# Cross-attention and a quantized feed-forward block: the feed-forward's quantized values turned by VectorE squares and a DMA through device memory instead of by TensorE

## The chip, the cores and the metric

The kernel runs on one core of a Trainium2 chip. The metric is the device time of one execution in microseconds (us); lower is better. Before the change the median of three executions is 2209.33 us (2207.35 to 2211.3).

## The reference, cut to what matters

```python
x = x + xattn(layernorm(x), ctx, ctx, Wq, bq, Wk, bk, Wv, bv, Wo, bo)   # x: 16 x 224 x 512, ctx: 16 x 750 x 512, 16 heads
x = x + ffn(layernorm(x), w_gate, w_up, w_down)

def fp4_quant_dequant(x):            # blocks of 16 along the last dimension
    scale = maximum(max(abs(xb)) / 6.0, 1e-12)
    idx = searchsorted(_MID, abs(xb / scale))
    return _GRID[idx] * sign(xb / scale) * scale

def fp4_linear(x, w):
    return einsum('bsk,nk->bsn', fp4_quant_dequant(x), fp4_quant_dequant(w))

def ffn(x, w_gate, w_up, w_down):    # 512 -> 1408 -> 512
    h = silu(fp4_linear(x, w_gate)) * fp4_linear(x, w_up)
    return fp4_linear(h, w_down)
```

## The kernel before, in words

The program has two stages, each a block of five instruction streams that run at their own pace and meet at semaphores. The first is the cross-attention over 16 batches (0 to about 1497 us in the trace); it also quantizes the three feed-forward weights and keeps gate and up turned and split in SBUF. The second is the feed-forward, `feed_forward`, over 28 tiles of 128 rows. All matrix products are made of three passes over operands that are split in a high and a low part (`PASSES`), so each operand is needed twice: the high part is written by ScalarE (a copy to float32r), the low part by VectorE (the value less the high part).

TensorE needs the quantized values with the contracted dimension on the partitions, so they are turned: the normed and quantized x of a tile (512 columns, 4 squares of 128) and the quantized hidden values (1408 columns, 11 squares of 128). Before the change TensorE turns them with an identity matrix into PSUM (`turn_x`, lines 1154 to 1162, and `turn_h`, lines 1185 to 1196), ScalarE copies the high parts out of `turn_bank` (lines 1216 to 1219 and 1233 to 1240), and VectorE subtracts (lines 1296 to 1299 and 1309 to 1315).

The order of work is written out by hand. `period_units(n)` gives the units of period n, and each engine walks that list and carries out what concerns it. In period n TensorE makes gate and up of tile n in three chunks of 512, 512 and 384 columns (`gate_up`, 24 matmuls a chunk) and the down product of tile n - 2 (`down`, 33 matmuls); VectorE quantizes in one pass of nine steps (`quant`, `quantize_step`) the hidden values of tile n - 1 together with the normed x of tile n + 2, 1920 columns in all, and between these steps makes the norm of tile n + 3, the hidden product of tile n (`hidden`, three chunks), the low parts, and the sum with the residual (`store`). ScalarE makes the silu of each chunk and the high parts. SyncE issues the transfers: `load` of a tile of x, `load_res` of the residual, `store` of the output. The banks for gate and up are two each, so `gate_up` of a chunk waits for the `hidden` of the chunk before the last one.

What a unit waits for can be said in counts: `gate_up(n, 0)` waits for `x_lo` of tile n, `down(n - 2, c)` for the low part of that chunk, `hidden(n, c)` for the silu, step 1 of `quant(n)` for `hidden(n - 1, 2)`.

Periods 3 to 24 are a hardware loop of two periods a turn (line 1096), the first three and the last five are written out. In periods 0 and 1 TensorE also turns the down weights.

## Time and profile before

| | before |
|---|---|
| median of three executions | 2209.33 us |
| the profiled execution's own time | 2209.99 us |
| its span, first to last instruction | 2208.2 us |
| PE busy | 2125.9 us (96%) |
| DVE busy | 1626.9 us (74%) |
| ACT busy | 866.9 us (39%) |
| feed-forward, from its first gate matmul | 1498.1 us to the end |
| granted TensorE clock, mean | 0.988 |

The page divides the span into 40 slices and shows for each engine its busy tenths; the timeline lists instructions in order of their start, neighbours of one kind merged; the windows sum busy time over a stretch. PE is the matmul part of TensorE, DVE is VectorE, ACT is ScalarE, SPq is the queue in which SyncE issues transfers. A start of one row less the start of the row before tells the pace, since neighbouring instructions overlap a little. "Landing" of a transfer is counted from its issue.

### The profile page before, as it was taken

How to read it: one execution, taken by the hardware profiler on the slowest of the kernel's cores; microseconds unless marked ns; L12 is line 12 of the kernel's file. 1: busy time of each engine (PE TensorE's matmuls, PEld its weight loads, DVE VectorE, ACT ScalarE, POOL GpSimd, SP SyncE). 2: the span in 40 equal slices, each digit the busy share in tenths (PEclk: the TensorE clock that was granted, in tenths of full speed). 3: DMA queues.
4: the chain of work that ended last, by engine and by line, in shares of the span. 5: the costliest groups of instructions: out<-in, count | busy, mean ns of one | idle time of the engine just before them, and what ended most of it. 6: DMA issues, size and time to landing. Idle time of an engine off the chain costs nothing. (4 is left out here: it accounts for less than half of the span.)

```text
span 2208.2 us, 43977 instructions
## 1 busy us (share of the span) xinstructions
PE 2125.9 (96%) x17252; PEld 1840.0 (83%) x17252; DVE 1626.9 (74%) x2818; ACT 866.9 (39%) x1805; POOL 96.5 (4%) x162
## 2 busy tenths in 40 slices
PE   4999999999999999999999999679999999999998
PEld 4888888888888988888889888558888888888886
DVE  4777777777777777776777777477878787788865
ACT  4554555455454554554545455342111111111111
POOL 0000000000000000000000000000000000000000
PEclk9999999999999999999999999879999999999999
DMA  5344444534434445345344444433000100010000
GB/s 163 102 113 105 124 106 122 136 94 116 131 94 123 104 122 132 98 120 136 93 118 105 122 124 104 109 103 95 29 28 28 43 28 28 28 39 33 24 20 29
DMA packets 124012, 197.24 MB, mean 89 GB/s; under 512 B 29776, under 2 KB 72272, under 8 KB 121280
## 3 DMA queue, kind: packets, MB, share of 16 engines
q1 hardware_dynamic: 123840, 194.86, 32.6%
q8 instruction: 118, 1.93, 0.4%
q14 instruction: 54, 0.44, 0.1%
HBM read 75.67 MB, written 23.33 MB: 45 GB/s over the span
## 5 line engine op out<-in xcount | busy, mean ns | idle before, releaser
L692 DVE TENSOR_REDUCE row_max<-max_bank 128x1 f32<-128x376 f32 (+1 forms) x896 | 450.7, 537 | 186.9 <-PE max_bank L523 186.5
L602 ACT ACTIVATE probs<-score_bank 125x448 f32<-125x448 f32 x768 | 399.5, 541 | 292.6 <-PE score_bank L537 289.8
L475 PE MATMUL proj_bank<-attention_operands 128*128 128x376 f32 (+1 forms) x1536 | 290.3, 338 | 24.5 <-DVE attention_operands L734 18.9
L497 PE MATMUL proj_bank<-attention_operands 128*128 128x256 f32 x2304 | 305.6, 283 | 6.1 <-DVE wo_lo L811 6.1
L537 PE MATMUL score_bank<-qstack,kstack 103*128 103x224 f32 x1536 | 301.0, 282 | 1.5 <-DVE qstack L703 1.3
L497 PEld LDWEIGHTS proj_bank<-attention_operands 128*128 128x128 f32 x2304 | 289.9, 190 | 6.4 <-DVE wo_lo L811 6.4
L537 PEld LDWEIGHTS score_bank<-qstack,kstack 103*128 103x128 f32 x1536 | 256.9, 192 | 37.8 <-issue 35.9
L475 PEld LDWEIGHTS proj_bank<-attention_operands 128*128 128x128 f32 x1536 | 264.1, 191 | 26.0 <-issue 18.9
L1231 ACT ACTIVATE f_act_gate<-gate_bank 128x512 f32<-128x512 f32 (+1 forms) x84 | 47.2, 562 | 504.4 <-PE up_bank L1181 504.4
L1181 PE MATMUL gate_bank<-gate_up,early 128*128 128x512 f32 (+1 forms) x1008 | 233.7, 381 | 1.5 <-PEq L1352 1.5
L1181 PE MATMUL up_bank<-gate_up,early 128*128 128x512 f32 (+1 forms) x1008 | 228.8, 376 | 0.0
L552 PE MATMUL pv_bank<-probs,values 125*32 125x224 f32 x3072 | 221.1, 360 | 0.0
L558 PE MATMUL pv_bank<-probs,ones 125*32 125x224 f32 x3072 | 217.2, 355 | 0.0
L1206 PE MATMUL down_bank<-ffn_down_hi,f_hqt 128*128 128x512 f32 x616 | 205.6, 400 | 6.5 <-DVE f_hqt L1314 6.5
L1181 PEld LDWEIGHTS up_bank<-gate_up,early 128*128 128x128 f32 x1008 | 184.9, 188 | 30.6
L1181 PEld LDWEIGHTS gate_bank<-gate_up,early 128*128 128x128 f32 x1008 | 181.0, 188 | 29.6 <-issue 2.0
L1307 DVE TENSOR_TENSOR f_hidden<-f_act_gate,up_bank 128x512 f32<-128x512 f32 (+1 forms) x84 | 54.0, 642 | 136.1 <-ACT f_act_gate L1231 136.1
L741 DVE RECIPROCAL heads<-pv_bank 128x112 f32<-128x112 f32 x128 | 108.6, 850 | 50.9 <-PE pv_bank L558 50.9
L1206 PEld LDWEIGHTS down_bank<-ffn_down_hi,f_hqt 128*128 128x128 f32 x616 | 116.6, 189 | 33.5 <-DVE f_hqt L1314 7.3
L558 PEld LDWEIGHTS pv_bank<-probs,ones 125*32 125x32 f32 x3072 | 100.4, 111 | 47.0 <-issue 2.0
L523 PE MATMUL max_bank<-early 128*128 128x376 f32 x448 | 131.7, 347 | 4.1 <-ACT early L640 2.3
L552 PEld LDWEIGHTS pv_bank<-probs,values 125*32 125x32 f32 x3072 | 87.3, 110 | 55.1 <-issue 19.0
(126 smaller groups left out, 2773.5 us busy)
## 6 DMA issues: line engine op xcount, KB each, us to landing
ctx_raw<-in_ctx SPq DMA_DIRECT2D x16, 1500.0 KB, 7.7
kstack<-k_low SPq DMA_DIRECT2D x256, 93.8 KB, 2.2
kstack<-early SPq DMA_DIRECT2D x256, 93.8 KB, 2.2
kstack<-k_high SPq DMA_DIRECT2D x256, 93.8 KB, 2.2
qstack<-early SPq DMA_DIRECT2D x384, 28.0 KB, 1.9
qstack<-q_part SPq DMA_DIRECT2D x384, 28.0 KB, 1.8
ffn_quant<-fw_share SPq DMA_DIRECT2D x48, 176.0 KB, 2.1
xn<-in_x SPq DMA_DIRECT2D x16, 448.0 KB, 9.9
```

What stands on the lines that cost most here:

```text
L475: last = nc.tensor.matmul(out[:, 0:hi - lo], w_hi_lo[W_K][ws][:, c, g * P:(g + 1) * P], ctx_part[cs][:, c, lo:hi], start=(n == 0), stop=(n ...
L497: last = nc.tensor.matmul(out[:, 0:256], ctx_part[cs][:, c, kt * KW:kt * KW + P], w_hi_lo[W_V][ws][:, c, half * 256:(half + 1) * 256], sta ...
L523: nc.tensor.matmul(out[:, 0:hi - lo], masked_columns[t % 2][:, m * P:(m + 1) * P], k_part[t % 2][0][:, lo:hi], start=True, stop=True).then ...
L537: last = nc.tensor.matmul(score_bank[j % 2][:, k * SQ:(k + 1) * SQ], kstack[t % 2][0:STK, j, kt * KW:kt * KW + P], qstack[t % 2][:, j, :], ...
L552: last = nc.tensor.matmul(pv_bank[j * DK:(j + 1) * DK, 0:SQ], values[:, t % NG // 2, kt, col:col + DK], probs[p][:, j, k, :], start=(kt == ...
L558: last = nc.tensor.matmul(pv_bank[j * DK:(j + 1) * DK, SQ:2 * SQ], ones[0:KW, :], probs[p][:, j, k, :], start=False, stop=(kt == KT - 1), ...
L602: nc.scalar.activation(probs[p][:, j, :, :], score_bank[j % 2][0:KW, 0:2 * SQ].rearrange("p (k q) -> p k q", k=2), ACT.Exp, scale=float(DK ...
L692: nc.vector.tensor_reduce(row_max[:, m, kh:kh + 1], mbank[:, 0:KSPLIT[kh + 1] - KSPLIT[kh]], AX.X, ALU.max).then_inc(max_reduced, 1)
L741: nc.vector.reciprocal(heads[:, half], pv_bank[:, SQ + half.start:SQ + half.stop])\
L1181: last = nc.tensor.matmul(banks[par][:, 0:w], xqt[n % 2][xs_][:, kc, :], ffn[m][ws][:, kc, chunk(c)], start=(k == 0), stop=(k == 11))
L1206: last = nc.tensor.matmul(down_bank[n % 2][:, :], hqt[hs][:, m, :], ffn[2][ws][:, m, :], start=(m == 0 and k == 0), stop=(m == FC - 1 and ...
L1307: nc.vector.tensor_tensor(hidden[:, chunk(c)], act_gate[par][:, 0:w], up_bank[par][:, 0:w], ALU.mult).then_inc(hidden_done, 1)
```

## The change

In the feed-forward's steady periods the turning leaves TensorE. After the ninth step of `quant(n)`, VectorE turns `quantized` in squares of 32 by 32 in one instruction into `strips` (unit `strips`). SyncE stores `strips`, 128 partitions of 1920 values, to a scratch in device memory, waits until it is there, and loads it back with four transfers of 32 partitions each into `turned`, so that the squares come to stand where the turned matrix has them (unit `bounce`). In the next period ScalarE makes the high parts from `turned` (`x_hi`, `h_hi`) and VectorE the low parts (`x_lo`, `h_lo`), both with SBUF as source instead of PSUM. `strips`, `turned` and the high and low parts of h are single buffers; the scratch has two.

The order in a period changes with it: the high parts stand at its head, the low parts behind the fourth step of `quant`, `hidden(n, 0)` behind the seventh, `hidden(n, 1)` and `strips` behind the ninth; TensorE makes all three chunks of `gate_up(n)` and then the three of `down(n - 2)`. All tiles are written out, with no hardware loop. The last two periods (28 and 29) turn by TensorE as before (`tail_units`). In the attention a table with explicit places replaces a sum of floats for the masks of q; the only effect is that in one of four slots a mask of q and `heads_hi` change places on ScalarE.

```diff
@@ period_units
-    return [*when(3, ("load", n + 3)), *when(0, ("gate_up", n, 0)), *quant(1, 2),
-            *when(-3, ("store", n - 3)), *quant(3, 4), *when(-1, ("load_res", n - 1)),
-            *when(1, ("turn_x", n + 1)), *when(-2, ("turn_h", n - 2, 0, has(1))),
-            *when(3, ("norm", n + 3)), *when(0, ("hidden", n, 0), ("gate_up", n, 1)),
-            *quant(5), *when(1, ("turn_x_lo", n + 1)), *quant(6), *when(-2, ("turn_h_lo", n - 2, 0)),
-            *when(-2, ("turn_h", n - 2, 1, has(1)), ("down", n - 2, 0), ("turn_h", n - 2, 2, has(1))),
-            *quant(7), *when(0, ("hidden", n, 1)), *when(-2, ("turn_h_lo", n - 2, 1)),
-            *when(3, ("normalize", n + 3)), *when(0, ("gate_up", n, 2)), *quant(8),
-            *when(-2, ("turn_h_lo", n - 2, 2)),  *when(0, ("hidden", n, 2)),
-            *when(-2, ("down", n - 2, 1), ("down", n - 2, 2)), *quant(9)]
+    spread = [("strips", n, has(-1), has(2))] if has(-1) or has(2) else []
+    bounce = [("bounce", n, has(-1), has(2))] if has(-1) or has(2) else []
+    return [*when(3, ("load", n + 3)), *when(1, ("x_hi", n + 1)), *when(-2, *[("h_hi", n - 2, c) for c in range(3)]),
+            *when(0, ("gate_up", n, 0)), *quant(1, 2, 3, 4),
+            *when(-2, *[("h_lo", n - 2, c) for c in range(3)]), *when(1, ("x_lo", n + 1)),
+            *quant(5, 6), *when(3, ("norm", n + 3)), *quant(7), *when(0, ("hidden", n, 0), ("gate_up", n, 1)),
+            *when(-3, ("store", n - 3)), *when(-1, ("load_res", n - 1)), *quant(8), *when(3, ("normalize", n + 3)), *quant(9),
+            *when(0, ("hidden", n, 1), ("gate_up", n, 2)), *(spread if last_spread is None or n <= last_spread else []),
+            *when(-2, *[("down", n - 2, c) for c in range(3)]), *when(0, ("hidden", n, 2)),
+            *(bounce if last_spread is None or n <= last_spread else [])]
...
@@ feed_forward
+    WC = W // P
+    in_squares = quantized[:, :].rearrange("p (k c j) -> p c k j", c=HG, j=DK)
+    strips = sb("f_strips", [P, HG, WC, DK])
+    turned = sb("f_turned", [P, HG, WC, DK])
...
-        with engine.Fori(1, tiles // 2 - 2) as i:
+        for i in range(1, tiles // 2 - 2):
             body(i, period_units(1) + period_units(2))
-        for n in range(1, 6):
-            body(tiles // 2 - 2, period_units(n, left=4 - n))
+        for n in range(1, 4):
+            body(tiles // 2 - 2, period_units(n, left=4 - n, last_spread=2))
+        for n in range(4, 6):
+            body(tiles // 2 - 2, tail_units(n))
...
@@ sync
+                elif kind == "bounce":
+                    part = chunks_of(*_rest)
+                    there = strips_dram[n % 2]
+                    sp.wait_ge(strips_made, tile + 1)
+                    reached(sp, turned_loaded, 16 * HG * (tile - 1))
+                    sp.dma_start(there.rearrange("p (c k j) -> p c k j", c=HG, j=DK)[:, :, part, :],
+                                 strips[:, :, part, :]).then_inc(strips_stored, 16)
+                    sp.wait_ge(strips_stored, 16 * (tile + 1))
+                    sp.wait_ge(x_lo, tile + 2)
+                    reached(sp, h_lo, 3 * (tile - 1))
+                    for c in range(HG):
+                        sp.dma_start(turned[c * DK:(c + 1) * DK, :, part, :], there.rearrange(
+                            "(g i) (c k j) -> c i g k j", i=DK, c=HG, j=DK)[bass.ds(c, 1), :, :, part, :].rearrange(
+                                "a i g k j -> (a i) g k j")).then_inc(turned_loaded, 16)
...
@@ scalar
+                if kind == "x_hi":
+                    act.wait_ge(turned_loaded, 16 * HG * (tile - 1))
+                    reached(act, gated, 3 * (tile - 1))
+                    nc.scalar.activation(in_strips(xqt[n % 2][0]), turned_chunks(FC, WC),
                                          ACT.Copy).then_inc(x_hi, 1)
+                elif kind == "h_hi":
+                    c = rest[0]
+                    q = 3 * tile + c
+                    if c == 0:
+                        act.wait_ge(turned_loaded, 16 * HG * (tile + 2))
+                        act.wait_ge(down_turned, FC)
+                    reached(act, down_part, q - 2)
+                    lo, hi = CH[c] // P, CH[c + 1] // P
+                    nc.scalar.activation(in_strips(hqt[0][:, lo:hi, :]), turned_chunks(lo, hi),
+                                         ACT.Copy).then_inc(h_hi, 1)
...
@@ vector
+                elif kind == "strips":
+                    part = chunks_of(*rest)
+                    dve.wait_ge(q_steps, quant_count(tile + 2, QSTEPS))
+                    reached(dve, strips_stored, 16 * tile)
+                    nc.vector.transpose(strips[:, :, part, :], in_squares[:, :, part, :]).then_inc(strips_made, 1)
+                elif kind == "x_lo":
                     dve.wait_ge(x_hi, tile + 1)
+                    nc.vector.tensor_tensor(in_strips(xqt[n % 2][1]), turned_chunks(FC, WC),
+                                            in_strips(xqt[n % 2][0]).bitcast(F32), ALU.subtract).then_inc(x_lo, 1)
+                elif kind == "h_lo":
+                    c = rest[0]
+                    dve.wait_ge(h_hi, 3 * tile + c + 1)
+                    lo, hi = CH[c] // P, CH[c + 1] // P
+                    nc.vector.tensor_tensor(in_strips(hqt[1][:, lo:hi, :]), turned_chunks(lo, hi),
+                                            in_strips(hqt[0][:, lo:hi, :]).bitcast(F32), ALU.subtract).then_inc(h_lo, 1)
```

VectorE's order from one period into the next, the kernel before, near its end (`f_q_steps` are the nine steps, L982 the ninth, L967, L969, L971 and L973 the first four, L1319 the sum with the residual):

```order
L982 TENSOR_TENSOR f_quantized<-f_round,f_scale 128x1920 [waits f_h_turned,f_x_turned,f_q_steps]
L967 TENSOR_REDUCE f_amax<-f_hidden 128x88 [waits f_hidden_done]
L969 TENSOR_SCALAR f_scale<-f_amax 128x88 [waits f_q_steps]
L1319 TENSOR_TENSOR f_res<-down_bank,f_res 128x512 [waits f_res_loaded1,f_down_part]
L971 RECIPROCAL f_inv_scale<-f_scale 128x88 [waits f_q_steps]
L973 SCALAR_TENSOR_TENSOR f_scaled<-f_hidden,f_inv_scale 128x1408 [waits f_q_steps]
```

The same place in the changed kernel, in a steady period (L986 is the ninth step, L971 the first, L979 the fifth, L1356 and L1350 the low parts, L1365 `hidden`; the waited names are in the diff):

```order
L986 TENSOR_TENSOR f_quantized<-f_round,f_scale 128x1920 [waits f_strips_made,f_q_steps]
L1365 TENSOR_TENSOR f_hidden<-f_act_gate,up_bank 128x512 [waits f_silu_done]
L1347 STREAM_TRANSPOSE f_strips<-f_quantized 128x1920 [waits f_strips_stored,f_q_steps]
L1365 TENSOR_TENSOR f_hidden<-f_act_gate,up_bank 128x384 [waits f_silu_done]
L971 TENSOR_REDUCE f_amax<-f_hidden 128x120 [waits f_hidden_done,f_x_normed]
L973 TENSOR_SCALAR f_scale<-f_amax 128x120 [waits f_q_steps]
L975 RECIPROCAL f_inv_scale<-f_scale 128x120 [waits f_q_steps]
L977 SCALAR_TENSOR_TENSOR f_scaled<-f_hidden,f_inv_scale 128x1920 [waits f_q_steps]
L1356 TENSOR_TENSOR f_hqt<-f_turned,f_hqt 128x512 [waits f_h_hi] x2
L1356 TENSOR_TENSOR f_hqt<-f_turned,f_hqt 128x384 [waits f_h_hi]
L1350 TENSOR_TENSOR early<-f_turned,early 128x512 [waits f_x_hi]
L979 TENSOR_SCALAR f_power<-f_scaled 128x1920 [waits f_q_steps]
```

Between the transpose and the first low part stand one `hidden` and four steps; before, no such instruction existed, and the low parts stood one by one between later steps.

SyncE's queue in a steady period of the changed kernel (L1179 the store of the strips, L1185 the four loads, L1160 the load of x, L1190 the output, L1172 the residual):

```order
L1179 DMA strips_scratch<-f_strips 128x1920 [waits f_turned_loaded,f_strips_made]
L1185 DMA f_turned<-strips_scratch 32x4x480 [waits f_h_lo,f_x_lo,f_strips_stored]
L1185 DMA f_turned<-strips_scratch 32x4x480 x3
L1160 DMA f_xn<-x_scratch 128x512 [waits f_x_normed]
L1190 DMA out<-f_res 128x512 [waits f_y_done]
L1172 DMA f_res<-x_scratch 128x512 [waits f_stored0]
```

ScalarE's queue over one period of the changed kernel (L1255 `x_hi`, L1265 `h_hi`, L1278 the silu):

```order
L1255 ACTIVATE early<-f_turned 128x512 [waits f_gate_up_made,f_turned_loaded]
L1265 ACTIVATE f_hqt<-f_turned 128x512 [waits f_down_part,f_down_turned,f_turned_loaded]
L1265 ACTIVATE f_hqt<-f_turned 128x512 [waits f_down_part]
L1265 ACTIVATE f_hqt<-f_turned 128x384 [waits f_down_part]
L1278 ACTIVATE f_act_gate<-gate_bank 128x512 [waits f_hidden_done,f_gate_up_made] x2
L1278 ACTIVATE f_act_gate<-gate_bank 128x384 [waits f_hidden_done,f_gate_up_made]
```

The five new transfers stand ahead of the load of x in SyncE's queue, and the two high parts that used to wait for TensorE's turning now wait for `turned_loaded`.

## Rows read from the trace of the kernel before

**Rows 1.** Page, part 2: TensorE and its clock in 40 slices of the span.
```profile
PE   4999999999999999999999999679999999999998
...
PEclk9999999999999999999999999879999999999999
```

**Rows 2.** Windows, steady part: stretch, busy us (instructions) by engine, clock, DMA share, GB/s.
```profile
1650.00:1700.00 50.00, 50.00 (x244) 42.21 (x243) 39.93 (x44) 7.35 (x14) 1.48 (x4) 1.00 0.10 31
```

**Rows 3.** Timeline, PE, one period: start us, us, engine, line, what, shapes, count.
```profile
1808.46 2.96 PE L1181 MATMUL gate_bank<-gate_up,early 128*128 128x512 f32 x12
1811.26 2.97 PE L1181 MATMUL up_bank<-gate_up,early 128*128 128x512 f32 x12
...
1824.03 2.33 PE L1181 MATMUL gate_bank<-gate_up,early 128*128 128x384 f32 x12
1826.19 2.24 PE L1181 MATMUL up_bank<-gate_up,early 128*128 128x384 f32 x12
...
1833.17 1.10 PE L1181 MATMUL gate_bank<-gate_up,early 128*128 128x512 f32 x4
```

**Rows 4.** Timeline, DVE, the same period.
```profile
1806.83 2.15 DVE L967 TENSOR_REDUCE f_amax<-f_hidden 128x120 f32<-128x1920 f32 x1
1809.01 0.22 DVE L969 TENSOR_SCALAR f_scale<-f_amax 128x120 f32<-128x120 f32 x1
...
1809.85 0.89 DVE L971 RECIPROCAL f_inv_scale<-f_scale 128x120 f32<-128x120 f32 x1
1810.78 2.16 DVE L973 SCALAR_TENSOR_TENSOR f_scaled<-f_hidden,f_inv_scale 128x1920 f32<-128x1920 f32 x1
1812.86 0.68 DVE L1264 BATCH_NORM_STATS2 f_stats<-f_xn 128x6 f32<-128x512 f32 x1
...
1815.67 1.15 DVE L975 TENSOR_SCALAR f_power<-f_scaled 128x1920 uint32<-128x1920 uint32 x1
1816.74 0.68 DVE L1298 TENSOR_TENSOR early<-turn_bank,early 128x512 fp32r<-128x512 f32 x1
1817.34 1.15 DVE L977 TENSOR_SCALAR f_power<-f_power 128x1920 f32<-128x1920 f32 x1
```

**Rows 5.** Timeline, ACT, the same period.
```profile
1815.32 0.61 ACT L1239 ACTIVATE f_hqt<-turn_bank 128x512 fp32r<-128x512 f32 x1
```

**Rows 6.** Groups by form, 100 to 1400: busy us, mean ns | idle before, releaser.
```profile
L734 DVE TENSOR_TENSOR attention_operands<-ctx_raw,attention_operands 128x750 fp32r<-128x750 f32 x60 | 52.4, 936 | 3.8 <-ACT attention_operands L633 3.8
...
L633 ACT ACTIVATE attention_operands<-ctx_raw 128x750 fp32r<-128x750 f32 x60 | 44.8, 818 | 0.4
```

**Rows 7.** DMA issues by line: KB each, median us from issue to landing.
```profile
ctx_raw<-in_ctx SPq DMA_DIRECT2D x16, 1500.0 KB, 7.7
kstack<-k_low SPq DMA_DIRECT2D x256, 93.8 KB, 2.2
...
f_res<-x_scratch SPq DMA_DIRECT2D x28, 256.0 KB, 2.6
out<-f_res SPq DMA_DIRECT2D x28, 256.0 KB, 2.0
...
values<-in_wk SPq DMA_DIRECT2D x1, 1024.0 KB, 6.1
```

**Rows 8.** Windows in a burst of 32-partition DMAs: us, DVE busy, clock, DMA share, GB/s.
```profile
124.00:126.00 2.00, 1.46 (x3) 1.00 0.65 152
...
140.00:142.00 2.00, 1.66 (x3) 1.00 0.56 203
```

**Rows 9.** Timeline, DVE, end of period 1.
```profile
1536.74 2.15 DVE L982 TENSOR_TENSOR f_quantized<-f_round,f_scale 128x1920 f32<-128x1920 f32 x1
```

**Rows 10.** Timeline, PE, last tiles' gate_up in period 27.
```profile
2169.48 2.34 PE L1181 MATMUL gate_bank<-gate_up,early 128*128 128x384 f32 x12
```

**Rows 11.** Timeline, PE, in the tail, behind an idle stretch.
```profile
2184.30 0.80 PE L1206 MATMUL down_bank<-ffn_down_hi,f_hqt 128*128 128x512 f32 x1 [4.63 <-DVE f_hqt L1314]
```

**Rows 12.** Windows, the stretch behind that idle time: columns as in Rows 2.
```profile
2184.00:2188.00 4.00, 3.70 (x9) 2.92 (x10) 3.91 (x4) 0.00 (x0) 0.00 (x0) 0.50 0.00 0
```

More of the change, by code:

```diff
@@ L73 @@
         "q": 7.96,
+        "mask": (8.26, 8.96, 9.66, 10.36),
         "q_lo": 8.16,
@@ L97 @@
         "q": 8.06,
+        "mask": (8.36, 9.06, 9.76, 10.46),
         "q_lo": 8.5,
@@ L121 @@
         "q": 8.7,
+        "mask": (9.0, 9.7, 10.4, 11.1),
         "q_lo": 11.71,
@@ L145 @@
         "q": 4.22,
+        "mask": (4.52, 5.22, 5.92, 6.62),
         "q_lo": 4.26,
@@ L226, in slot_units @@
         add(at["q_lo"], ("q_lo", g + 2))
-        add((at["q"] + 0.3, at["q"] + 1.0, at["q"] + 1.7, at["q"] + 2.4), *[("mask_q", g + 2, j) for j in range(HG)])
+        add(at["mask"], *[("mask_q", g + 2, j) for j in range(HG)])
         ahead, half = g // 2, 1 - g // 2
@@ L982, in quantize_step, with period_units @@
     return dve.tensor_tensor(blocks(out), blocks(t), spread(scale), ALU.mult)
-def period_units(n, first=None, left=None):
+def period_units(n, first=None, left=None, last_spread=None):
     def has(k):
@@ L1031, in with_down, with feed_forward @@
     return out + [("down_turn_lo", i) for i in turns if ("down_turn_lo", i) not in out]
-def feed_forward(nc, ctx, x1, out, ffn, ident, ln_consts, tiles, ffn_quant, xqt, fs):
+def feed_forward(nc, ctx, x1, out, ffn, ident, ln_consts, tiles, ffn_quant, strips_dram, xqt, fs):
     def sb(name, shape, dt=F32):
@@ L1153, in body @@
                 tile = 2 * i + n
-                if kind == "turn_x":
-                    reached(pe, q_steps, quant_count(tile, QSTEPS))
-                    reached(pe, x_lo, tile)
-                    reached(pe, h_lo, 3 * (tile - 4) + 2)
-                    for c in range(KC):
-                        col = F + c * P
-                        last = nc.tensor.transpose(turn_bank[0][:, c * P:(c + 1) * P], quantized[:, col:col + P],
-                                                   ident[:, :])
-                    last.then_inc(x_turned, 1)
-                elif kind == "down_turn":
+                if kind == "down_turn":
                     pe.wait_ge(down_loaded[n % RAWS], 16 * (n // RAWS) + 16)
@@ L1185, in body @@
                 elif kind == "turn_h":
-                    c, after_x = rest
+                    c = rest[0]
                     q = 3 * tile + c
-                    reached(pe, q_steps, quant_count(tile + 3, QSTEPS))
-                    reached(pe, h_lo, q - 1 if c else q)
-                    if c == 1 and after_x:
-                        reached(pe, x_lo, tile + 4)
+                    pe.wait_ge(q_steps, quant_count(tile + 3, QSTEPS))
+                    pe.wait_ge(h_lo, q - 1 if c else q)
                     for m in range(CH[c] // P, CH[c + 1] // P):
@@ L1281, in body @@
                             reached(dve, hidden_done, 3 * tile)
-                    if step == QSTEPS and with_x:
-                        reached(dve, x_turned, tile + 2)
-                    if step == QSTEPS and with_h:
-                        reached(dve, h_turned, 3 * (tile - 1))
+                    if step == QSTEPS and (with_x or n < 4):
+                        reached(dve, strips_made, tile)
+                    elif step == QSTEPS:
+                        dve.wait_ge(h_turned, 3)
                     cols = slice(0 if with_h else F, W if with_x else F)
@@ L1327, in cross_attention_ffn @@
     ffn_raw = [dram[n] for n in ("gate", "up", "down")]
+    strips_dram = [nc.dram_tensor(f"strips{i}_scratch", (P, F + D), F32, kind="Internal").ap() for i in range(2)]
     ffn_quant = [nc.dram_tensor(f"ffn_quant{n}", w.shape, F32, kind="Internal").ap() for n, w in enumerate(ffn_raw)]
@@ L1356, in cross_attention_ffn @@
         with ExitStack() as ctx:
-            feed_forward(nc, ctx, x1, out, [*gate_up, down], ident, ln_consts, batches * SQ // P, ffn_quant, xqt, fs)
+            feed_forward(nc, ctx, x1, out, [*gate_up, down], ident, ln_consts, batches * SQ // P, ffn_quant, strips_dram, xqt, fs)
 def kernel(x, ctx_1024, L0_xattn_Wq, L0_xattn_bq, L0_xattn_Wk, L0_xattn_bk, L0_xattn_Wv, L0_xattn_bv,
```

26 lines of the change are left out of this document (18 added, 8 removed).

## The prediction

> **What bounds the kernel now.** I read the page's slices first: PE is at nine tenths in nearly every one and its clock at full level [rows 1]. Then the windows of the steady feed-forward: in 50 us PE is busy 50.00, DVE 39.93, ACT 7.35, at clock 1.00 and 31 GB/s of DMA [rows 2]. So TensorE bounds this stage, and there is no gap to fill, only work to remove. The PE timeline gives the period: gate_up of one tile starts at 1808.46, of the next at 1833.17, so 24.71 us [rows 3]. A half chunk of twelve 512-wide matmuls takes 2.80 (1808.46 to 1811.26), which is 0.233 each; the 384-wide ones take 2.16 and 2.1 (2.24 less the overlap of 0.16). The matmuls alone are 4 x 2.80 + 2.16 + 2.1 + 33 x 0.233 = 23.1. The rest of the period, 1.6, is the 15 transposes. DVE's work in a period is 39.93 / 50 x 24.71 = 19.7.
>
> **What the change removes.** The transposes of the steady periods: 1.6 us each in the queue that sets the end. Nothing hides them, so on PE's side this would give 1.6 x some 25 periods = 40 us, if PE stayed the bound.
>
> **What it adds to DVE.** One square transpose of 1920 columns a period. No row shows one. The nearest rows are quantization steps over the same 1920 columns: 1.15 for the simplest, 2.15 for the others [rows 4]. Below, 1.1 is one bound; above I take two passes, 4.3. I take 2.15, since it reads and writes every element once as those steps do. DVE then has 19.7 + 2.1 = 21.8 of work, still under 23.1. The low parts keep their price: 128x750 from SBUF takes 0.936 against 0.68 for 512 from PSUM, and 238 columns less at the step rate (2.15 per 1920) are 0.27, so 0.67 [rows 4, 6]. The same holds for ACT: 0.818 for 750, so about 0.6 for 512, as 0.61 now [rows 5, 6].
> The Trainium skill (VectorE: DVE Perf Modes, The three transpose paths) gives 311 ns for a 128x128 block in 2-byte values on VectorE. Fifteen such blocks would be an estimated 4.7 us, in place of 2.15; by that the sum below would be some 65 us more, near the two-pass rival. No run here shows it.
>
> **What it adds to the path.** This is where I expect the time to go. In period n, ACT's first unit waits for the load of bounce n - 1; DVE's low parts of h wait for ACT; and DVE executes in order, so steps 5 to 9, hidden(n, 0), hidden(n, 1) and strips(n) all queue behind them. Strips(n) starts bounce n. That closes a loop from one strips to the next, with the whole bounce in it, and all DVE has to do meanwhile is hidden(n - 1, 2), 0.5 by its 384 columns, and steps 1 to 4, together 0.5 + 2.18 + 0.24 + 0.93 + 2.08 = 5.9 us [rows 4]. The loop, step by step:
> - Bounce B. Strips made to issue, 0.2. Store of 960 KB: a store of 256 KB lands in 2.0, and a load of 1500 KB lands in 7.7 against 2.6 for 256, so 4.1 us per 1000 KB; 2.0 + 704 x 0.0041 = 4.9. Wait and issue, 0.2. Load of 960 KB in four pieces of 32 partitions: in a burst of such DMAs, mixed with others, at most 203 GB/s move in 2 us [rows 8]; 983 thousand bytes at that are 4.8, and the fixed part is 2.6 - 1.1 = 1.5 (256 KB move in 1.1 at 4.1 per 1000 KB), together 6.3. The last piece is no later than that by issue: a 94 KB piece lands in 2.2 [rows 7]. Semaphore to ACT, 0.1. B = 0.2 + 4.9 + 0.2 + 6.3 + 0.1 = 11.7.
> - Landing to step 5. x_hi 0.6, then h_hi(0) 0.6, then DVE 0.1 later: three h_lo at a pace of 0.6, 0.6 and 0.5 (512, 512 and 384 columns) and x_lo 0.6 (1816.74 to 1817.34): 3.6 in all [rows 4, 5].
> - Step 5 to the end of strips: 1.2 + 1.07 for steps 5 and 6 (1815.67 to 1816.74; the sixth waits for the fifth), norm 0.9 (0.68 and a short second instruction), step 7 2.07, hidden 0.6, sum with the residual 0.6, step 8 2.07, normalize 0.5 (512 columns, no longer than a subtraction), step 9 2.07, hidden 0.6, transpose 2.15 = 13.8 [rows 4].
> The period is T = B + 17.4 = 29.1 us, against 24.7 now: the gain of 1.6 on PE is void and 4.4 are added. PE idles 6 us a period, in one gap ahead of gate_up(n, 2), which waits for hidden(n, 0). Behind hidden(n, 0), PE has 4.2 + 7.7 + 5.6 + 5.6 = 23.1 before it needs the next one, so it never sets T. The third chunk's silu is done 5 us after hidden(n, 0), and DVE comes to hidden(n, 2) 8.6 after it: covered.
> On pricing the bounce, a rule weighs in. The Trainium skill (SBUF — State Buffer, Door 1: The DMA port swizzle) says that DMA speed goes with the SBUF ports reached, and 32 partitions reach only 8 of 16, about 218 GB/s. With its fixed 2 us this makes the load an estimated 6.5 and the store (all ports, 436 GB/s) 4.3. The sum would be B = 11.3, 10 us less at the end. Its point speaks against the change: splitting the load by partitions halves its speed.
>
> **Clock.** In the tail PE idles 4.63 before 2184.30 [rows 11], and in the 4 us that follow its granted clock is 0.50, the 1.2 GHz level [rows 12]; then it is back at 2.4. If each gap of 6 us brings the same 4 us at half pace, PE loses 2 us a period: 25.1, still under 29.1. I price it at nothing; cover is those 4 us, and if T fell under 25.1 it would count.
>
> **Other edits.** The load of x now stands behind the bounce in SyncE's queue; it lands with it, and norm comes 5.9 us later: nothing. Output and residual loads are issued before the strips are made: nothing. No loop: PE shows no idle at its turns (50.00 of 50), so 0; more instructions to fetch, but the attention stage is straight-line already. The mask that changes places on ACT: neither instruction is longer than 0.6, so over 15 batches it could give or cost 9 us at most; in the table both had places far behind what they wait for, so I take 0.
>
> **The sum.** In period 1 the ninth step ends at 1538.9 [rows 9]; the transpose comes behind it, less the work that now stands behind it: strips(1) ends at 1540. Bounce 0 (x only) is done long before period 1 needs it. Then 24 full loops (n = 2 to 25): 24 x 29.1 = 698, so 2238.4. Loop 26 quantizes 1408 columns and has no norm: 29.1 - 3.9 = 25.2, so 2263.6. In period 27: a bounce of 704 KB, 9.5; high part and three h_lo 2.4; steps 5 to 7, 3.3, and hidden 0.7: gate_up(27, 2) starts at 2279.5. Now it starts at 2169.48 [rows 10]: 110.0 later. From there to the end took 2208.2 - 2169.5 = 38.7. In the new tail: 4.2 and down(25) 7.7; turn, copy, subtract 1.8; down(26) with its last turn 8.0; wait for step 9, 1.0; turn, copy, subtract 1.8; down(27) 8.0; sum and output 3.1 = 35.6. Span 2279.5 + 35.6 = 2315.1; with the 1.8 between span (2208.2) and own time (2209.99), **2317 us**. The profiled execution lies 0.7 above the median, within the spread of the runs, so I leave it. Per us of B the time moves by 26 us.
>
> **The range of this case.** B lower: 1024 KB land in 6.1 and 1500 in 7.7 [rows 7], 3.4 us per 1000 KB, for both legs: 0.9 + 3.3, 1.5 + 3.3, 0.5 = 9.5, so 2317 - 57 = 2260. B upper: the burst's other window moved 152 GB/s [rows 8]; a load at that is 8.0, and a store half as much slower again 6.5, so 15: 2403.
>
> **Rivals.**
> - Faster: the bounce hides. If the two legs were priced like those of 256 KB, 2.0 and 2.6, B would be about 5, and with B under 5.7 T falls to PE's 23.1 and the kernel takes 2210 - 40 - 2 = 2168. It breaks even at B = 11.7 - 107/26 = 7.6. For it: each small transfer does land so. Against it: 960 KB each way, and 1024 KB have a row of 6.1 for one leg alone. Chance 0.03.
> - Slower transfers: the bounce's rows of 1920 bytes and its 32 partitions move at 152 GB/s in both directions or worse: B = 15.8, time 2424. Chance 0.12.
> - The transpose takes two passes, 4.3: 26 x 2.15 = 56 more, 2373. Chance 0.12.
> - The clock stays at 1.2 GHz through whole periods: PE then needs 46.2 a period, 24 x 17.1 = 410 more, 2727. Against it: it returned within 4 us in the tail. Chance 0.02.
> - My forecast, with its own range 2260 to 2403: 0.70. Within 0.2% of before: 0.01.
>
> **The numbers.** The range 2260 to 2400 leaves out the slow transfers (0.12), the hidden bounce, no change and the clock (0.06 together), and holds the two-pass transpose. A measurement of this kernel tells apart some 0.2%. Faster by more 0.03, within 0.01, slower 0.96.
>
> **What would show it.** In the new profile: DVE idle some 7 us a period before the first h_lo, released by ACT's f_hqt copy, and ACT idle before x_hi released by the DMA f_turned<-strips_scratch; the issue of the store landing in about 5, the last load in about 6; transposes of about 2.15; PE idle some 6 a period before the gate matmuls of chunk 2, released by f_hidden; period 29.1. Wrong would be: PE without gaps at a period of 23.1, or a DVE without idle time whose transposes are long.

## The result, and the profile after

The changed kernel takes 2291.31 us, the median of four executions (2289.6 to 2298.37). The kernel before takes 2208.34 in four executions beside it (2207.2 to 2211.3). The ratio is 1.0386, with an interval of 1.037 to 1.0402: 83 us slower, where the forecast was 108 slower (2317 in a range of 2260 to 2400).

| | before | after |
|---|---|---|
| profiled execution's own time | 2209.99 us | 2289.6 us |
| span | 2208.2 us | 2287.8 us |
| PE busy | 2125.9 (96%) | 2124.5 (93%) |
| DVE busy | 1626.9 (74%) | 1681.7 (74%) |
| granted TensorE clock, mean | 0.988 | 0.967 |

The page's slices of the changed kernel, against [rows 1]:

```profile
PE   4999999999999999999999997687888889888898
...
PEclk9999999999999999999999999798999999999999
```

From the 27th slice on, in the feed-forward, PE is mostly at eight tenths, where it was at nine. The attention part looks as before: the first gate matmul of the feed-forward starts at 1495.26, where it started at 1498.10, and in the other runs below this start lies between 1493.8 and 1504.2. The page's fourth part, the chain that ended last, by engine in shares of the span; the first line is the kernel before, the second the changed one:

```profile
PE 30%; DVE 2%; issue 0%; ACT 0%; DVEq 0%
DVE 15%; DMA 11%; issue 4%; PE 3%; SPq 1%; ACT 1%; ACTq 0%; DVEq 0%
```

PE falls from 30% of the span to 3%, and DVE and DMA together have 26%: the chain that ends last no longer runs through TensorE in the feed-forward. Its groups by line (busy us, mean ns of one | idle time before them, releaser):

```profile
L1219 PE MATMUL gate_bank<-gate_up,early 128*128 128x512 f32 (+1 forms) x1008 | 263.9, 418 | 83.5 <-DVE f_hidden L1365 82.0
...
L1356 DVE TENSOR_TENSOR f_hqt<-f_turned,f_hqt 128x512 fp32r<-128x512 f32 (+1 forms) x78 | 45.8, 643 | 154.9 <-ACT f_hqt L1265 154.9
...
L1255 ACT ACTIVATE early<-f_turned 128x512 fp32r<-128x512 f32 x26 | 16.4, 632 | 306.9 <-DMA f_turned<-strips_scratch 306.9
```

ScalarE waits 306.9 us for the loads of `turned`. DVE waits 154.9 us ahead of the first low part (L1356), released by ScalarE's copy, and PE waits 82.0 for `hidden`. In windows of the steady part (stretch, busy us of PE, PEld, DVE, ACT, POOL, then clock, DMA share, GB/s; compare [rows 2]):

```profile
1600.00:2000.00 400.00, 355.62 (x1494) 298.49 (x1494) 306.50 (x311) 53.81 (x103) 35.83 (x28) 0.92 0.35 99
1668.66:1672.66 4.00, 4.00 (x23) 4.00 (x24) 4.00 (x4) 0.00 (x0) 0.00 (x0) 1.00 0.28 85
1754.42:1758.42 4.00, 4.00 (x16) 4.00 (x17) 4.00 (x4) 0.00 (x0) 0.00 (x0) 0.68 0.29 98
1809.97:1813.97 4.00, 4.00 (x14) 4.00 (x15) 4.00 (x4) 0.00 (x0) 0.00 (x0) 0.57 0.24 83
1837.40:1841.40 4.00, 4.00 (x14) 4.00 (x15) 4.00 (x4) 0.00 (x0) 0.00 (x0) 0.57 0.29 96
```

PE has 355.62 of 400 us, and DVE is not full either, with 306.50. No engine bounds this stage; a loop of waits does. One period on DVE (start us, us, what, idle time before and its releaser), to set beside [rows 4]:

```profile
1815.53 2.17 DVE L1347 STREAM_TRANSPOSE f_strips<-f_quantized 128x1920 f32<-128x1920 f32 x1
...
1818.24 2.15 DVE L971 TENSOR_REDUCE f_amax<-f_hidden 128x120 f32<-128x1920 f32 x1
...
1821.63 2.16 DVE L977 SCALAR_TENSOR_TENSOR f_scaled<-f_hidden,f_inv_scale 128x1920 f32<-128x1920 f32 x1
1829.16 1.76 DVE L1356 TENSOR_TENSOR f_hqt<-f_turned,f_hqt 128x512 fp32r<-128x512 f32 x3 [5.38 <-ACT f_hqt L1265]
1830.84 0.69 DVE L1350 TENSOR_TENSOR early<-f_turned,early 128x512 fp32r<-128x512 f32 x1
1831.44 1.15 DVE L979 TENSOR_SCALAR f_power<-f_scaled 128x1920 uint32<-128x1920 uint32 x1
```

The transpose (L1347) takes 2.17. Behind it come one `hidden` and steps 1 to 4 (the first of them at 1818.24, the fourth until 1823.8), and then nothing for 5.38 us until the high part is there. The same bounce in SyncE's queue (L1179 the store, L1185 the four loads, L1160 the load of x) and on ScalarE:

```profile
1817.73 0.32 SPq L1179 DMA_DIRECT2D strips_scratch<-f_strips  x1
1821.44 1.74 SPq L1185 DMA_DIRECT2D f_turned<-strips_scratch  x4
1823.23 0.43 SPq L1160 DMA_DIRECT2D f_xn<-x_scratch  x1
```

```profile
1827.98 0.63 ACT L1255 ACTIVATE early<-f_turned 128x512 fp32r<-128x512 f32 x1 [11.49 <-DMA f_turned<-strips_scratch]
```

Strips are made at 1817.70. The store is issued at 1817.73, the loads 3.71 later at 1821.44, once the store has landed, and ScalarE starts x_hi 6.54 after that, at 1827.98. The bounce is 10.28 here. The transfers by issue (KB each, median us from issue to landing), beside [rows 7]:

```profile
strips_scratch<-f_strips SPq DMA_DIRECT2D x25, 960.0 KB, 3.7
f_turned<-strips_scratch SPq DMA_DIRECT2D x100, 240.0 KB, 4.6
...
f_xn<-x_scratch SPq DMA_DIRECT2D x26, 256.0 KB, 5.4
```

And PE, against [rows 3]:

```profile
1809.97 3.78 PE L1219 MATMUL gate_bank<-gate_up,early 128*128 128x384 f32 x12 [3.24 <-DVE f_hidden L1365]
...
1837.40 3.89 PE L1219 MATMUL gate_bank<-gate_up,early 128*128 128x384 f32 x12 [2.55 <-DVE f_hidden L1365]
...
1843.22 0.39 PE L1242 MATMUL down_bank<-ffn_down_hi,f_hqt 128*128 128x512 f32 x1
```

PE idles in one gap a period, always ahead of the gate matmuls of chunk 2, which wait for `hidden`. Here the gap is 3.24 and 2.55 us; over 20 periods it is 1.93 to 6.08, 3.1 in the mean. The twelve matmuls behind these two gaps take 3.78 and 3.89, where [rows 3] has 2.33; the last two windows above show the clock granted in those 4 us, 0.57, so mostly the lower level. Not every gap has that behind it: the second and third window stand behind gaps of 1.93 and 1.94 us, and the clock is 1.00 in one and 0.68 in the other.

### The profile page after: what moved, and what is told of

Same layout as the page of the kernel before. It is cut to its first block and busy times, and to the rows that moved or that the text cites. A ratio compares the mean times of both kernels' runs of the same rounds, so it can differ in the third digit from the quotient of the medians.

```text
span 2287.8 us, 42311 instructions
## 1 busy us (share of the span) xinstructions
PE 2124.5 (93%) x16862; PEld 1834.5 (80%) x16862; DVE 1681.7 (74%) x2845; ACT 868.0 (38%) x1805; POOL 140.4 (6%) x162
## 5 line engine op out<-in xcount | busy, mean ns | idle before, releaser
L1219 PE MATMUL gate_bank<-gate_up,early 128*128 128x512 f32 (+1 forms) x1008 | 263.9, 418 | 83.5 <-DVE f_hidden L1365 82.0
L1219 PEld LDWEIGHTS gate_bank<-gate_up,early 128*128 128x128 f32 x1008 | 213.1, 218 | 124.3 <-issue 94.2
L1219 PE MATMUL up_bank<-gate_up,early 128*128 128x512 f32 (+1 forms) x1008 | 236.3, 385 | 0.0
L1219 PEld LDWEIGHTS up_bank<-gate_up,early 128*128 128x128 f32 x1008 | 194.2, 197 | 30.6
L1242 PE MATMUL down_bank<-ffn_down_hi,f_hqt 128*128 128x512 f32 x616 | 197.8, 394 | 1.9 <-DVE f_hqt L1372 1.9
L1278 ACT ACTIVATE f_act_gate<-gate_bank 128x512 f32<-128x512 f32 (+1 forms) x84 | 46.6, 556 | 333.9 <-PE up_bank L1219 333.9
L1356 DVE TENSOR_TENSOR f_hqt<-f_turned,f_hqt 128x512 fp32r<-128x512 f32 (+1 forms) x78 | 45.8, 643 | 154.9 <-ACT f_hqt L1265 154.9
L1255 ACT ACTIVATE early<-f_turned 128x512 fp32r<-128x512 f32 x26 | 16.4, 632 | 306.9 <-DMA f_turned<-strips_scratch 306.9
```

The costliest lines, as they stand in the source:

```text
L1219: last = nc.tensor.matmul(banks[par][:, 0:w], xqt[n % 2][xs_][:, kc, :], ffn[m][ws][:, kc, chunk(c)], start=(k == 0), stop=(k == 11))
L1242: last = nc.tensor.matmul(down_bank[n % 2][:, :], hqt[hs][:, m, :], ffn[2][ws][:, m, :], start=(m == 0 and k == 0), stop=(m == FC - 1 and ...
L1356: nc.vector.tensor_tensor(in_strips(hqt[1][:, lo:hi, :]), turned_chunks(lo, hi), in_strips(hqt[0][:, lo:hi, :]).bitcast(F32), ALU.subtract ...
```

## The experiments

Each ran beside the kernel before on one chip, and "us" is a median: of two executions where the store or the transpose is made twice in section 1 and for the doubled store in section 3, of four to twelve elsewhere. In the measurements below, "the period" is the mean distance from one transpose's start to the next and "the bounce" the mean time from the end of `strips` to the start of x_hi, both between 1600 and 2150 us, some 20 periods of each trace. In the changed kernel these are 28.04 and 10.88, the latter 3.96 from store to first load and 6.89 from there to x_hi. The theory is that of the prediction: one in-order loop, in which each us of bounce costs 26 us of the kernel. The rivals are that DMA or DVE is simply too busy (the windows of the changed kernel have DMA at 0.35 and DVE at 306.50 of 400), that the DMA bounce costs by itself wherever its consumer stands, and that the straight-line code or the mask table costs something.

### 1. Is it in the loop: the store twice, and the transpose twice

The store is made twice, one after the other, each waited for:

```diff
-                    sp.dma_start(there.rearrange("p (c k j) -> p c k j", c=HG, j=DK)[:, :, part, :],
-                                 strips[:, :, part, :]).then_inc(strips_stored, 16)
-                    sp.wait_ge(strips_stored, 16 * (tile + 1))
+                    for twice in range(2):
+                        sp.dma_start(there.rearrange("p (c k j) -> p c k j", c=HG, j=DK)[:, :, part, :],
+                                     strips[:, :, part, :]).then_inc(strips_stored, 16)
+                        sp.wait_ge(strips_stored, 16 * (2 * tile + twice + 1))
```

> The changed kernel with the strips stored twice, one store after the other, each waited for. Theory: the bounce is 3.7 to 3.8 longer in each of 26 loops: 2291 + 98 = 2389, between 2380 and 2400. Rival (the transfers are covered by DVE's work): 2291 within 5.

Measured: 2385.75 us (ratio 1.0815, 1.0791 to 1.0838), 94 more than the changed kernel. SyncE's queue, where the two stores are one row:

```profile
1824.77 4.48 SPq L1180 DMA_DIRECT2D strips_scratch<-f_strips  x2
1832.62 1.75 SPq L1186 DMA_DIRECT2D f_turned<-strips_scratch  x4
```

The bounce is 14.56, 3.68 longer than 10.88, and the period 31.68, 3.64 longer than 28.04. Some 26 such periods make 95. The time of a transfer stands in the period us for us.

The second transpose, behind the first one:

```diff
-                    sp.wait_ge(strips_made, tile + 1)
+                    sp.wait_ge(strips_made, 2 * tile + 2)
...
+                    nc.vector.transpose(strips[:, :, part, :], in_squares[:, :, part, :]).then_inc(strips_made, 1)
+                    dve.wait_ge(strips_made, 2 * tile + 1)
```

> The changed kernel with the transpose made twice on VectorE. Theory: the transpose is in the same loop, 2.15 x 26 = 56 more: 2347, between 2340 and 2352. Rival (DVE has idle time that takes it up): 2291 within 5.

Measured: 2344.63 us (ratio 1.0628, 1.0605 to 1.0651), 53 more. On DVE:

```profile
1812.61 2.17 DVE L1347 STREAM_TRANSPOSE f_strips<-f_quantized 128x1920 f32<-128x1920 f32 x1
1814.81 2.18 DVE L1349 STREAM_TRANSPOSE f_strips<-f_quantized 128x1920 f32<-128x1920 f32 x1
...
1828.56 1.76 DVE L1358 TENSOR_TENSOR f_hqt<-f_turned,f_hqt 128x512 fp32r<-128x512 f32 x3 [5.48 <-ACT f_hqt L1265]
```

DVE still idles 5.48 ahead of L1358, the low parts, though it has 2.2 us more to do. The period is 30.05, 2.0 longer, and 26 x 2.0 = 52. So it is not the amount of DVE's work that costs; the work stands in the loop. By the same slope the one transpose that the change adds would cost the kernel an estimated 53 us; no run leaves it out.

### 2. Where the consumer stands: high parts behind the silu, low parts behind step 8

```diff
@@ period_units
-    return [*when(3, ("load", n + 3)), *when(1, ("x_hi", n + 1)), *when(-2, *[("h_hi", n - 2, c) for c in range(3)]),
-            *when(0, ("gate_up", n, 0)), *quant(1, 2, 3, 4),
-            *when(-2, *[("h_lo", n - 2, c) for c in range(3)]), *when(1, ("x_lo", n + 1)),
+    return [*when(3, ("load", n + 3)), *when(0, ("gate_up", n, 0)),
+            *when(1, ("x_hi", n + 1)), *when(-2, *[("h_hi", n - 2, c) for c in range(3)]), *quant(1, 2, 3, 4),
...
-            *when(-3, ("store", n - 3)), *when(-1, ("load_res", n - 1)), *quant(8), *when(3, ("normalize", n + 3)), *quant(9),
+            *when(-3, ("store", n - 3)), *when(-1, ("load_res", n - 1)), *quant(8),
+            *when(-2, *[("h_lo", n - 2, c) for c in range(3)]), *when(1, ("x_lo", n + 1)),
+            *when(3, ("normalize", n + 3)), *quant(9),
```

> The changed kernel with the consumers of the bounce moved later in the period: DVE's low parts stand behind the eighth step instead of the fourth, and on ACT the silu of chunk 0 stands ahead of the high parts. Nothing is added or removed. Theory (the bounce lies in DVE's queue, only 5.9 us of work stand ahead of its consumers): now 14.4 us of DVE work follow the transpose before the first low part, the bounce and the high part take 10.9 + 1.2 = 12.1, so DVE never waits, and the period falls from 28.0 to TensorE's 23.1: 2291 - 24 x 4.8 - some 4 = about 2171, which is also 38 below the kernel before; 2165 to 2182. Rival (DVE's own work with the transpose is the bound, or the SBUF sources or the clock are): it stays above 2260.

Measured: 2209.31 us (ratio 1.0016, 1.0002 to 1.0029). That is 82 less than the changed kernel and near the kernel before, but not the 2171 expected, nor in its range of 2165 to 2182: the expectation missed. DVE, and SyncE's queue for the same period:

```profile
1818.83 1.16 DVE L981 TENSOR_SCALAR f_power<-f_power 128x1920 f32<-128x1920 f32 x1
1822.53 0.69 DVE L1312 BATCH_NORM_STATS2 f_stats<-f_xn 128x6 f32<-128x512 f32 x1 [2.54 <-DMA f_xn<-x_scratch]
```

```profile
1815.23 1.74 SPq L1186 DMA_DIRECT2D f_turned<-strips_scratch  x4
1817.02 0.43 SPq L1161 DMA_DIRECT2D f_xn<-x_scratch  x1
```

The wait ahead of the low parts is gone, and the next one in the queue shows: the norm of tile n + 3 (L1312) waits 2.54 us for the load of its x, which SyncE issues at 1817.02 behind the four loads of the bounce, and which lands only 5.5 later. It had its slack from the wait that was removed. The loop now runs from strips through the store and the issue of the loads to the load of x, the norm, steps 7 to 9 with the units between them, and strips: the bounce's store is still in it. PE still waits for `hidden`:

```profile
1826.23 2.32 PE L1220 MATMUL gate_bank<-gate_up,early 128*128 128x384 f32 x12 [1.41 <-DVE f_hidden L1366]
```

To see which of the two moved units acts, only ScalarE's order was changed:

```diff
@@ period_units
-    return [*when(3, ("load", n + 3)), *when(1, ("x_hi", n + 1)), *when(-2, *[("h_hi", n - 2, c) for c in range(3)]),
-            *when(0, ("gate_up", n, 0)), *quant(1, 2, 3, 4),
+    return [*when(3, ("load", n + 3)), *when(0, ("gate_up", n, 0)),
+            *when(1, ("x_hi", n + 1)), *when(-2, *[("h_hi", n - 2, c) for c in range(3)]), *quant(1, 2, 3, 4),
```

> The changed kernel with one half of that edit: ACT makes the silu of chunk 0 ahead of the high parts, DVE's order is kept. Theory: DVE's low parts still stand behind the fourth step, the loop is the same: 2291 within 4. Rival (ACT, blocked by the load, holds up the silu and with it hidden and TensorE): it falls by 20 or more.

Measured: 2340.98 us (ratio 1.0608, 1.0586 to 1.0631), 50 more than the changed kernel; the expectation missed. PE, then ScalarE, then DVE in one period:

```profile
1800.53 4.18 PE L1219 MATMUL gate_bank<-gate_up,early 128*128 128x384 f32 x12 [4.34 <-DVE f_hidden L1365]
...
1814.60 2.96 PE L1219 MATMUL gate_bank<-gate_up,early 128*128 128x512 f32 x12
...
1830.31 4.18 PE L1219 MATMUL gate_bank<-gate_up,early 128*128 128x384 f32 x12 [4.34 <-DVE f_hidden L1365]
```

```profile
1820.40 0.60 ACT L1278 ACTIVATE f_act_gate<-gate_bank 128x512 f32<-128x512 f32 x1 [12.80 <-PE up_bank L1219]
1820.89 0.62 ACT L1255 ACTIVATE early<-f_turned 128x512 fp32r<-128x512 f32 x1
```

```profile
1822.07 1.76 DVE L1356 TENSOR_TENSOR f_hqt<-f_turned,f_hqt 128x512 fp32r<-128x512 f32 x3 [7.73 <-ACT f_hqt L1265]
...
1829.48 0.68 DVE L1365 TENSOR_TENSOR f_hidden<-f_act_gate,up_bank 128x512 f32<-128x512 f32 x1
```

ScalarE is held by the silu of the next tile's first chunk (12.80 released by PE's up_bank), and x_hi follows it at once with no wait for the DMA. So this loop has no DMA in it. From the gate matmuls of chunk 2, 1800.53, it goes through the down product to the first chunk of the next tile at 1814.60 (14.07), to its silu at 1820.40 (5.80), to the first low part at 1822.07 (1.67), to `hidden` at 1829.48 (7.41) and to the gate matmuls again at 1830.31 (0.83): 29.78, where the mean period is 29.89. In this loop PE's work counts, and so does its clock. Behind the gap of 4.34 it is at its lower level, 1.2 GHz:

```profile
1800.53:1804.53 4.00, 4.00 (x13) 4.00 (x14) 4.00 (x4) 0.00 (x0) 0.00 (x0) 0.50 0.33 83
```

The twelve matmuls take 4.18 where [rows 3] has 2.33. Chunk 2 and the down product take 14.07, where the prediction has 4.2 + 7.7 = 11.9 for them at the full clock: 2.2 of the 29.8 us are the lower clock. The other half alone, the low parts late and ScalarE's order kept, was not run, so what each half is worth by itself is not shown.

### 3. The consumer late and the load of x early

Against the kernel of the first diff of section 2, the load of x moves ahead of the bounce, one tile earlier:

```diff
@@ period_units
-    return [*when(3, ("load", n + 3)), *when(0, ("gate_up", n, 0)),
+    return [*when(0, ("gate_up", n, 0)),
...
-            *when(-3, ("store", n - 3)), *when(-1, ("load_res", n - 1)), *quant(8),
+            *when(-3, ("store", n - 3)), *when(-1, ("load_res", n - 1)), *when(4, ("load", n + 4)), *quant(8),
@@ ffn_start_units
-    return [("load", 2)] + [("down_load", i) for i in range(RAWS)] + [("norm", 2), ("normalize", 2)]
+    return [("load", 2), ("load", 3)] + [("down_load", i) for i in range(RAWS)] + [("norm", 2), ("normalize", 2)]
```

> The kernel of e1 with the load of x issued one period earlier, ahead of the bounce in SyncE's queue instead of behind it. Theory: what held e1 at a period of 24.7 to 25.3 was VectorE's norm, which waited 2.5 to 3.1 us for that load (issued 5.5 us behind the strips' store, on queues full of the bounce); with it gone DVE's loop is its work, 22.0, and TensorE's 23.1 is the bound: 2209 - 25 x 1.7 = 2168, between 2160 and 2180, below the kernel before. Rival (some other wait of e1 is next, or the clock): 2195 or more.

Measured: 2169.04 us (ratio 0.9811, 0.9797 to 0.9825): 122 less than the changed kernel and 39 less than the kernel before. It beats both, with the same bounce. The window and SyncE's queue:

```profile
1600.00:2000.00 400.00, 400.00 (x1826) 336.63 (x1825) 380.49 (x384) 63.36 (x121) 43.51 (x34) 1.00 0.41 120
```

```profile
1806.73 0.43 SPq L1161 DMA_DIRECT2D f_xn<-x_scratch  x1
1813.85 0.32 SPq L1180 DMA_DIRECT2D strips_scratch<-f_strips  x1
1817.54 1.74 SPq L1186 DMA_DIRECT2D f_turned<-strips_scratch  x4
```

PE has 400.00 of 400 at clock 1.00. The load of x (L1161) goes out 7.1 ahead of the store, and lands sooner, in 2.9 against 5.4 in the transfers of the changed kernel:

```profile
f_xn<-x_scratch SPq DMA_DIRECT2D x26, 256.0 KB, 2.9
```

On DVE the norm (L1312) waits for nothing, and neither do the low parts (L1357). DVE now waits 0.90 for a silu, since PE is the bound:

```profile
1822.21 0.68 DVE L1312 BATCH_NORM_STATS2 f_stats<-f_xn 128x6 f32<-128x512 f32 x1
...
1826.05 0.69 DVE L1366 TENSOR_TENSOR f_hidden<-f_act_gate,up_bank 128x512 f32<-128x512 f32 x1 [0.90 <-ACT f_act_gate L1279]
...
1829.32 1.76 DVE L1357 TENSOR_TENSOR f_hqt<-f_turned,f_hqt 128x512 fp32r<-128x512 f32 x3
```

Neither DMA nor DVE was too busy: DMA's share is now 0.41 and DVE's work 380.49 of 400, more than in the changed kernel. The period is 23.07 (gate matmuls of chunk 2 at 1807.75 and 1830.82), 1.64 under the 24.71 of before, and 24 x 1.64 = 39 is the gain. The bounce moved as many bytes, and from strips to x_hi it is even longer, 12.05, because x_hi stands behind a silu.

The two additions of section 1, made to this kernel, test the same statement from the other side. The store twice:

> The kernel of e10 with the strips stored twice. Theory: landing and high parts then end 10.9 + 3.8 + 1.3 = 16.0 us behind the transpose, against 14.4 us of VectorE work: it waits 1.6, the period is 22.0 + 1.6 = 23.6, so 12 us above e10 (0 to 25 above), where the same edit cost 94 on the changed kernel. Rival (a longer bounce costs in full wherever its consumers stand): 90 or more above e10.

Measured: 2172.55 us (ratio 0.9832, 0.9813 to 0.9851), 3.5 more, where the same edit cost 94 in the changed kernel. The two intervals overlap, so even these 3.5 are not shown: in the traces the feed-forward, from its first gate matmul to the end, takes 669.65 us with the doubled store (from 1503.25 to 2172.9) and 669.5 without (from 1499.70 to 2169.2). The low parts now just miss their cover:

```profile
1814.55 1.76 DVE L1358 TENSOR_TENSOR f_hqt<-f_turned,f_hqt 128x512 fp32r<-128x512 f32 x3 [0.69 <-ACT f_hqt L1267]
```

That wait of 0.69 falls into DVE's slack against PE, and PE stays at 400.00 of 400. The transpose twice:

> The kernel of e10 (2169) with the transpose made twice on VectorE. Theory: in e10 TensorE bounds with 23.1 a period and VectorE has 22.0 of work; with a second transpose VectorE has 24.1 and takes over as the bound, 1.0 more a period: 2169 + 25 = 2194, between 2185 and 2205. The same edit cost 53 on the changed kernel, where the transpose lay in the loop in full. Rival (VectorE has more slack than its busy time says): 2175 or less.

Measured: 2197.87 us (ratio 0.9959, 0.9944 to 0.9974), 29 more. Here the amount of DVE's work does decide:

```profile
1600.00:2000.00 400.00, 383.70 (x1732) 318.27 (x1731) 394.00 (x380) 61.15 (x118) 42.10 (x34) 1.00 0.38 113
```

DVE has 394.00 of 400, the profile shows it one wait in these 400 us, of 0.5, and the period is 24.30 in nearly every case: DVE is the bound, and PE waits some 1.0 a period. 24 x (24.30 - 23.07) = 30.

### 4. What the load's time is made of

The loads of pieces 2 and 3 go out from ScalarE's queue, with the same waits:

```diff
-                    for c in range(HG):
+                    for c in range(2):
...
+                if kind == "bounce":
+                    act.wait_ge(strips_stored, 16 * (tile + 1))
+                    act.wait_ge(x_lo, tile + 2)
+                    reached(act, h_lo, 3 * (tile - 1))
+                    for c in range(2, HG):
+                        nc.scalar.dma_start(turned[c * DK:(c + 1) * DK, :, part, :], there.rearrange(
...
```

> The changed kernel with the four loads of the bounce issued from two queues, partitions 0 to 63 from SyncE, 64 to 127 from ScalarE, at the same time. If the load is held by the SBUF ports that 32 partitions reach, the two halves run side by side and the load falls from 6.7 to about 4.5: 26 x 2.2 = 57 less, 2234. If it is held by the issue of four transfers in a row (0.43 each), 1 us less: 2265. If by the engines' rate for pieces of 1920 bytes: 2291 within 5.

Measured: 2270.51 us (ratio 1.0271, 1.0254 to 1.0287), 21 less, nearest to the expectation for the issuing. First load to x_hi is 6.14 against 6.89, and the bounce 10.01 against 10.88: 0.87 x 26 = 23. The pieces, by the queue that issues them (KB each, median us from issue to landing):

```profile
f_turned<-strips_scratch SPq DMA_DIRECT2D x50, 240.0 KB, 4.1
f_turned<-strips_scratch ACTq DMA_DIRECT2D x50, 240.0 KB, 4.9
```

SyncE's four issues took 1.74 us, its two take 0.79, so the last piece is issued 0.9 sooner, and x_hi starts 0.75 sooner. A piece still needs 4.1 or 4.9, where the four had a median of 4.6: two queues save the issuing and little of the moving. In the other experiment SyncE alone issues them, in another order:

```diff
-                    for c in range(HG):
+                    for c in (0, 2, 1, 3):
```

> The changed kernel with the same four loads from SyncE alone, in the order of partitions 0, 64, 32, 96 instead of 0, 32, 64, 96. If what the two queues won came from both halves of the partitions being written at once, neighbours in the one queue overlap too and it gains 5 to 20: 2271 to 2286. If it came from the issue by two sequencers or from the second queue, nothing: 2291 within 4.

Measured: 2285.31 us (ratio 1.0346, 1.0329 to 1.0363), 6 less; the interval only just leaves that of the changed kernel (1.037 to 1.0402). The bounce is 10.56, 0.32 shorter, and 0.32 x 26 = 8. The time lies at the edge of the 2271 to 2286 expected for halves of the partitions that overlap, and the direction fits them; but a load at twice the speed would give 2 us a period and more. What sets the load's 6.7 us was not settled: issue order is worth 0.3, a second queue 0.75 (0.9 of the whole bounce), and the rest stays open.

### 5. The other parts of the change alone

The kernel before, with its loop written out and the table for the masks, and nothing else:

```diff
-        add((at["q"] + 0.3, at["q"] + 1.0, at["q"] + 1.7, at["q"] + 2.4), *[("mask_q", g + 2, j) for j in range(HG)])
+        add(at["mask"], *[("mask_q", g + 2, j) for j in range(HG)])
...
-        with engine.Fori(1, tiles // 2 - 2) as i:
+        for i in range(1, tiles // 2 - 2):
```

> The kernel before with the two other parts of the change alone: all tiles written out instead of the hardware loop, and the table of places for the masks. Theory: neither is worth anything, 2209 within 4. Rival (part of the 83 us comes from code fetched anew, or from the attention's order): 2215 or more.

Measured: 2210.93 us over twelve executions (ratio 1.001, 0.9999 to 1.0021): no difference. In its trace PE is busy 400.00 of 400 us in the same steady window, as before, and the feed-forward takes 710.05 us from its first gate matmul to the end, where it took 710.1. The two parts were not run one by one.

## Why the prediction was right, and where it was off

- **What bounded before, and what leaves.** Right. The 1.6 us a period of PE's transposes are void in the changed kernel and come out as 1.64 where the loop is opened (section 3).
- **The transpose.** Taken at 2.15, the price of a step over the same columns; measured 2.17. The rival of two passes fell. So did the sum by the Trainium skill (VectorE: DVE Perf Modes, The three transpose paths): by its 311 ns for a block of 128x128 in 2-byte values 15 blocks would be an estimated 4.7, and the one wide instruction over fp32 values takes 2.17.
- **DVE's work, 21.8 a period.** Right, and not the bound: in the opened kernel 380.49 of 400 over a period of 23.07 is 21.9.
- **The store, 4.9, and 0.2 behind it.** This is the term that was mis-sized. From store to first load it is 3.96 in the mean: 3.7 in most periods, 4.1 to 5.7 in some. It was built up from a store of 256 KB with the slope of loads.
- **The load, 6.3, and 0.1 to ScalarE.** A little low: 6.89 in the mean, 6.7 in most periods. With 0.03 before the store in place of 0.2, the bounce is 10.88 and not 11.7. The estimates by the Trainium skill (SBUF — State Buffer, Door 1: The DMA port swizzle, and for the fixed 2 us The DMA setup-cost knee), 4.3 and 6.5, were nearer on both legs; its rule that a load by 32 partitions reaches half the ports is in line with a load that takes longer than the store of the same bytes, 6.7 against 3.7. No run here separates the ports from other causes of that; mixing the halves in section 4 gained 0.3.
- **The rest of the period, 17.4.** Landing to step 5 was 3.6 and is 3.46 (1827.98 to 1831.44), step 5 to the end of strips 13.8 and 13.69 (to 1845.13). With the mean bounce of 10.88 the mean period leaves 17.2 for the two. So T is 28.0, not 29.1.
- **The sum.** Strips(1) ends at 1537.66, not 1540. With 24 loops and the short last one it put the gate matmuls of chunk 2 in period 27 at 2279.5; they start at

```profile
2250.89 2.26 PE L1219 MATMUL gate_bank<-gate_up,early 128*128 128x384 f32 x12
```

  which is 28.6 sooner: 2.3 from the start, and 1.1 us in each of some 24 loops. The 2.3 are luck, since in this execution the attention ended 2.8 sooner than in the trace that the forecast started from. From there to the end it is 36.9 (forecast 35.6). 2317 - 28.6 + 1.3 = 2289.7, the profiled 2289.6.
- **26 us per us of bounce.** Shown in both directions: 3.68 more gave 94, 0.87 less gave 21.
- **"PE idles 6 us a period".** Wrong in its kind. PE idles 3.1 in the mean (1.9 to 6.1), and the rest of the difference, 5.82 for chunk 2 from 1837.40 to 1843.22 against 4.26 at the full clock, is work at half pace. The prediction had worked out those 2 us and then did not take them off the idle time. The total was not touched.
- **"DVE idle some 7 us a period".** It is 154.9 us over 26 periods, 6.0 each, in the place and with the releaser that were forecast; the shorter bounce accounts for 0.8 of the difference.
- **The clock at nothing.** Right for this kernel, where PE is outside the loop. Wrong as soon as the loop passes through PE: 2.2 us of each period in the second kernel of section 2.
- **The load of x at nothing.** Right, and it holds only because of the wait ahead of it. With that wait gone it cost 40 us, 2209.31 against 2169.04. The prediction said that norm comes 5.9 us later; it did not say that this was the load's cover.
- **Break-even at a bounce of 7.6.** Not reached by any run, so only the slope of 26 stands behind it. The faster rival, 2168, came true by another road: the bounce took as long as ever and had other work beside it.

## What to carry to other kernels

In this kernel the round trip through memory was priced by where its consumer stands in the in-order queues: its length counted us for us where it was longer than the work beside it, and no cost was shown where it was not. So count the work that each engine can do between the producer and the first instruction that waits: with 5.9 us of it the kernel lost 83 us, and with some 15 us (1813.74 to 1829.32 in the kernel of section 3), and the load of x moved ahead, it gained 39. Before moving that consumer, write down what else was hiding in its wait: the load of x behind the bounce took back the whole gain over the kernel before (40 us), and the silu moved ahead alone made the kernel 50 us slower. An addition made twice, in both orders of the queue, tells a loop (94 us for the store, 53 for the transpose) from a bound by an engine's work (no difference shown for the store, 29 for the transpose).
